# A graph layer's source gather: 48 of 420 columns made by TensorE instead of 39, named sooner, fetched a group ahead

## The reference, cut to what matters

```python
def _L1_gnn_ref(feat, W1, W2, b, src, dst):
    out_deg = jnp.maximum(segment_sum(ones, src), 1.0)
    t1 = feat @ W1
    msg = t1[src] + feat[src] * feat[dst] @ W2
    msg = msg / (sqrt(out_deg[src]) * sqrt(out_deg[dst]))[:, None]
    agg = jax.ops.segment_sum(msg, dst, num_segments=n)
```

## Time and profile before

| | us |
|---|---|
| median of three runs (lowest, highest) | 2574.71 (2570.63, 2580.15) |
| span of the profiled execution | 2204.9 |
| the stage of the change, from its first to its last sums | 1105.0 to 1596.8 |
| its first and last gather by GpSimd | 1105.7 and 1588.4 |
| its first and last matmul of L2323 | 1157.6 and 1592.5 |

### The profile page before, as it was taken

One profiled execution on the slowest core, in us unless ns is written; L12 is line 12 of the kernel. 1 busy time (PEld: TensorE's weight loads), 2 busy tenths in 40 slices (PEclk: granted clock), 3 DMA queues, 4 the chain that ended last, 5 costly groups with the idle time before them and its releaser, 6 DMA issues. The chain is left out here.

```text
span 2204.9 us, 38514 instructions
## 1 busy us (share of the span) xinstructions
PE 1760.4 (80%) x11779; PEld 1497.5 (68%) x11780; DVE 1277.6 (58%) x2754; ACT 873.7 (40%) x1797; POOL 1173.9 (53%) x1179
## 2 busy tenths in 40 slices
PE   5737988878775899699708878878778699999996
PEld 4525766666654777588607767666657599999995
DVE  7337977777768633346667788877638722222221
ACT  4425765555553244322142222222225634333332
POOL 2667777777770400056567777777640045444442
PEclk9958987777887899899959898999978699999998
DMA  3588655555565362567567866666650566767775
GB/s 93 137 181 199 169 162 151 154 156 150 157 150 131 79 181 80 140 198 226 181 192 248 263 225 224 222 219 219 214 157 24 181 208 192 203 187 192 199 188 146
DMA packets 203516, 384.67 MB, mean 174 GB/s; under 512 B 43525, under 2 KB 138170, under 8 KB 203199
## 3 DMA queue, kind: packets, MB, share of 16 engines
q1 hardware_dynamic: 136871, 223.77, 33.5%
q0 software_dynamic: 65696, 157.37, 26.8%
q10 hardware_dynamic: 840, 2.16, 0.3%
HBM read 277.93 MB, written 108.69 MB: 175 GB/s over the span
## 5 line engine op out<-in xcount | busy, mean ns | idle before, releaser
L808 POOL DMA_INDIRECT qr<-q_rows,src_t x415 | 407.4, 982 | 126.5 <-issue 124.1
L2303 POOL DMA_INDIRECT fr<-pair_rows,dst_i x381 | 363.0, 953 | 123.6 <-issue 113.1
L2323 PE MATMUL psP<-f_part,onehot 125*128 125x256 bf16 x2925 | 359.8, 286 | 85.2 <-DVE onehot L2349 85.1
L2323 PEld LDWEIGHTS psP<-f_part,onehot 125*128 125x128 bf16 x2925 | 297.2, 103 | 141.2 <-DVE onehot L2349 95.1
L906 PE MATMUL psK<-kp,oh_k 126*128 x1680 | 281.5, 332 | 94.1 <-DVE qr L1011 66.1
L906 PEld LDWEIGHTS psK<-kp,oh_k 126*128 126x128 bf16 x1680 | 191.4, 115 | 164.8 <-issue 99.8
L2361 DVE SCALAR_TENSOR_TENSOR psA<-psA,same,fr 128x256 f32<-128x256 f32 x420 | 206.5, 492 | 75.0 <-DMA fr<-pair_rows,dst_i 42.9
L2443 ACT ACTIVATE acc<-psA 128x1280 f32<-128x1280 f32 x84 | 103.9, 1237 | 331.0 <-DVEq L2364 310.8
L1919 ACT ACTIVATE m1hT<-m1psH,m1par 128x128 f32<-128x128 f32 x448 | 127.7, 368 | 252.7 <-PE m1psH L1939 252.7
L1939 PEld LDWEIGHTS m1psH<-m1xT,n_rows 128*128 128x128 f32 x1792 | 208.7, 192 | 5.0 <-DMA n_rows<-in_L_ffn_W_dram 1.2
L1939 PE MATMUL m1psH<-m1xT,n_rows 128*128 128x128 f32 x1792 | 209.3, 275 | 1.7 <-DMA n_rows<-in_L_ffn_W_dram 1.1
(11 more groups left out here) (502 smaller groups left out, 2685.1 us busy)
## 6 DMA issues: line engine op xcount, KB each, us to landing
n_rows<-in_L_ffn_W_dram SPq DMA_DIRECT2D x56, 1024.0 KB
run_rows<-acc SPq DMA_DIRECT2D x84, 640.0 KB
loc<-locals_ SPq DMA_DIRECT2D x85, 157.5 KB
ea<-in_edge_attr_dram SPq DMA_DIRECT2D x84, 140.0 KB
w_first<-in_L_ffn_Wd_dram SPq DMA_DIRECT2D x8, 1024.0 KB, 11.8
w_all<-in_L_ffn_W_dram SPq DMA_DIRECT2D x8, 1024.0 KB, 10.3
m1b<-in_L_ffn_b_dram SPq DMA_DIRECT2D x56, 128.0 KB, 2.9
qr<-q_rows,src_t POOLq DMA_INDIRECT x420
```

What stands on the lines that cost most here:

```text
L808: nc.gpsimd.indirect_dma_start(out=qr[:, n % GQ, u, :], out_offset=None, in_=q_rows, in_offset=bass.IndirectOffsetOnAxis(ap=src_t[:, n, u: ...
L2303: nc.gpsimd.indirect_dma_start(out=fr[:, n % GI, u, :], out_offset=None, in_=f_rows, in_offset=bass.IndirectOffsetOnAxis(ap=f_at[:, n * G ...
L2323: last = nc.tensor.matmul(psP[:, k % 2, 0:D], onehot[:, k % 2, t, :], f_part[:, c, t, :], start=(t == 0 and c == 0), stop=(t == T - 1 and ...
```

## The change

TensorE makes 48 columns. `PG` is now (7, 9, 10, 12, 14, 15, 17, 18, ..., 79, 80, 82): 28 of the distances between neighbours are two groups and 19 are one. Group 83 has no such column any more. Column k+1 is named after tile 6 of column k, not 12. ScalarE in turn n fetches the product for group n+1, if there is one, ahead of the copy of group n. The source numbers as floats lie in `dst_f`, a buffer that is free by then; one VectorE instruction makes them for all 84 groups, not for 39. The place of `one_hots` in VectorE's program, two groups ahead of use, is as before.

```diff
-        PG = tuple(range(7, NK, 2))
-        NP = len(PG)
+        NP = 48
+        PG = tuple(7 + (2 * i + 1) * (NK - 8) // (2 * NP) for i in range(NP))
-            cols7 = sb(st, "cols7", [E, NP])
+            cols7 = dst_f[:, 0:NK]
-                        if t == T // 2 and k + 1 < NP:
+                        if t == T // 4 and k + 1 < NP:
                             name_sources(k + 1)
-                nc.vector.tensor_copy(cols7[:], src_i[:, PG[0] * G + G - 1::2 * G]).then_inc(s_cols7, 1)
+                nc.vector.tensor_copy(cols7[:], src_i[:, G - 1::G]).then_inc(s_cols7, 1)
-                    nc.scalar.activation(col_wide[:, k % CR, :], cols7[:, k:k + 1].to_broadcast([E, P]), ACT.Copy).then_inc(s_colb, 1)
+                    nc.scalar.activation(col_wide[:, k % CR, :], cols7[:, PG[k]:PG[k] + 1].to_broadcast([E, P]), ACT.Copy).then_inc(s_colb, 1)
                 for n in range(NK):
-                    if n in PG:
-                        k = PG.index(n)
+                    if n + 1 in PG:
+                        k = PG.index(n + 1)
                         if k + 3 < NP:
                             widen(k + 3)
                         act.wait_ge(s_pe7, k + 1)
-                        act.wait_ge(s_free7, n - GI + 1)
-                        nc.scalar.activation(fr[:, n % GI, G - 1, :], psP[:, k % 2, 0:D], ACT.Copy).then_inc(s_pek7, 1)
+                        act.wait_ge(s_free7, n + 1 - GI + 1)
+                        nc.scalar.activation(fr[:, (n + 1) % GI, G - 1, :], psP[:, k % 2, 0:D], ACT.Copy).then_inc(s_pek7, 1)
```

## The result

| | before | changed | |
|---|---|---|---|
| median of 17 runs each, us | 2574.71 | 2556.0 | ratio 0.9926, 95% interval 0.9906 to 0.9947 |
| lowest, highest | 2565.35, 2590.62 | 2543.6, 2586.45 | |
| forecast | | 2565.4 (2557 to 2581) | |

The changed kernel's highest time is of a slow run, which the ratio leaves out. The mechanism that the prediction gave is not the one at work.

The account below looks back on a forecast made before the run. GpSimd's gathers were taken to bound the stage, ending it at 1583.9, the VectorE-TensorE chain at 1583.5; with 2 us added, 1585.9 against 1595.25 is 9.3 us less: 2574.7 becomes 2565.4 us, range 2557 to 2581.

Parts of the forecast that it names:

- With the 369.8 us around it as before: Last step, whole kernel: 369.8 us outside the span stay, so a span of 2195.6 us gives a median of 2565.4.
- It waits for nobody ... GpSimd is saturated.: Stage of the change: GpSimd's gathers cost 1.256 us each and set the pace; only 7.6 us are waits for VectorE.
- the 11.3 of the sum: GpSimd in the stage: nine gathers go at 1.256 us each, 11.3 us, with no cover.
- A column is 8.41 us.: TensorE in the stage: 8.41 us from naming to naming with nothing waited for, naming included.
- The early name: VectorE's one-hot: ready 6.2 us into a column, not 8.2, sparing VectorE 2 us in each of 19 places.
- The fetch ahead: ScalarE's fetch: removes VectorE's 9.0 us wait in 35 places, worth nothing before, needed now; possible delay taken as 0.
- nearly gone: Sign of being right, in the stage: VectorE's wait for the fetched column, 9.0 us in 35 places, nearly vanishes.
- those listed as wrong: Stage: GpSimd waiting for VectorE over 5 us beyond the start, mid-column naming waiting for fetch, copies awaiting TensorE, 10 us columns.
- those listed as right: Stage: 372 gathers with 0.30 us issue, last at 1577; VectorE's gather wait under 15 us; last sums at 1585 to 1587.
- A: Chain through VectorE and TensorE: 0.3 to 0.5 us per hand-over in 48 columns; 2582 us, at half 2573; chance 0.20.
- B's low clock: TensorE: 16 columns start at the low clock, 26.7 us on the chain; 15 us later than before, 2589.7; chance 0.10.
- C's wait for landed rows: Gathers in the stage: landing, not issue, sets the pace; gain 3 us, 2572; chance 0.10.

Follow-up runs that it names:

- before again: The kernel before, unchanged, profiled once more in the condition in which the change was timed; 2579.75 us beside 2582.2, ratio 0.9992.
- the second pair: The changed kernel against the same kernel without the fetch a group ahead (48 columns, named after tile 6); both 0.9926 of before, the latter 2568.78 us beside 2588.3.
- the waiting kernel: The changed kernel with GpSimd's gathers of group n waiting for TensorE's product of group n-2; 2217.17 us, 1.0011 of before, which took 2215.37 on that chip.

## Why the prediction was wrong

The step that failed is "With the 369.8 us around it as before", on which the reading of every row rests. In each of the runs here the device time is 1.7 to 2.1 us above the span of the same execution, so the 369.8 us between the median and the span of the first profile did not lie around it. It meant that the profiled execution ran at another pace than the timed ones, and that the rows described a condition in which the change was not going to be timed. Most of the rest follows.

- **"It waits for nobody ... GpSimd is saturated."** True of the profile read, and at that pace the price of a gather held within a fifth (44.0 against 39.9 to 43 us, 28.9 against 24 to 26). In the timed condition GpSimd waits 156.3 us for VectorE. Nine gathers less with the name as before (48 columns only) gave 7 us, 0.3 to 13.7; this does not exclude the 11.3 of the sum.
- **"A column is 8.41 us."** From first to last matmul it is 8.3 us in the median of the first profile, 13.0 in before again (27 of 39 over 11), 11.1 in the changed kernel (25 of 48), and 8.3 with one gather a group.
- **The early name, taken at 0 beside columns a group apart** (it only kept 2 us in 19 places from being lost). This is the mis-sized step behind the gain: alone it gave 19 us (12.7 to 25.3), as much as the change.
- **The fetch ahead, at 0.** Right in size: 0.9999 alone, and the ratio is 0.9926 with and without it. The prediction also called it needed in a tight chain; that the second pair doesn't show.
- **VectorE's wait for fetched columns "nearly gone".** It rose, 90.3 to 123.6 us. Its wait for gathers did fall below 15 us, but it was so in before again too.
- **The signs.** Of those listed as wrong, three stand in the profile after: GpSimd waits for VectorE (147.5 us, bound 5), columns of 10 us and more (11.1 in the median), and a naming that waits for the fetch in the middle of a column (25.5 us in nine places, and 60.7 us with the early name alone). Of those listed as right: 372 gathers with 0.28 us of "issue" each, but the last at 1921.9.
- **The rivals.** None was this. A (a price at each hand-over) is nearest in kind, but its sign was the other: in the timed condition before paid such a price already, and the change pays less of it (VectorE waits 206.3 us for names and products in before again, 150.0 in the changed kernel). B's low clock has a part, but is not the cause: in before again matmuls that follow each other at about twice the full-speed distance add 51 us to the columns (27 in the first profile), the stalls of over 0.5 us 176, and with one gather a group two of these stalls are left. The earlier trace rows already had a full-speed column behind a wait of 2.76 us, so a wait of over 2.1 us does not decide it alone. C's wait for landed rows is in neither profile of this pace.

So the right sign was luck: it came of a wrong model, and the gain of a part that the sum had at 0. What stays open: by what path the gathers hold TensorE back; whether TensorE's matmuls or only the signals are late in a stall (both kinds of rows are above); why one kernel takes 2215 us on one chip and 2580 on others; whether the changed kernel gains its 11 us at the faster pace; and whether holding GpSimd back helps at the slower one.

## What to carry to other kernels

Compare the profiled execution's span with the timed median before using a row: here a gap of 14% meant that another condition was timed, and its waits had to be profiled first. Where an engine stalls within its unit of work, move what others wait for to the front of the unit; here that was worth more than cutting the engine's work (19 us for the name, nothing for a third of the matmuls). A change of position tried as a series (tiles 18, 12, 6, 2) shows the cause as a dose, which a single edit does not.

## What the runs showed of the hardware

At the slower pace, TensorE's progress depends on GpSimd's indirect gathers. Some gathers after a pause its loads and matmuls come singly, in the stretch shown at multiples of 0.7 us; a column is 11.1 us (changed kernel) or 13.0 us (before again) long in the median, for 8.3. Late product signals arrive 2.8 us in the median (1.0 to 3.1, changed kernel) after the last gather began. With a quarter of the gathers all but two of 105 stalls are gone, and with rows an eighth as long they stay. At the faster pace gathers at the same rate do none of it: no late signal with 39, 16 or 4 columns, nor in the waiting kernel with 48.

Is TensorE short of instructions in these stalls? The Trainium skill (Runtime: NRT & Kernel Launch, "Instruction fetch mechanics") says that an engine fetches its instructions in blocks of 16 KiB by a DMA queue of its own, and that this is mostly hidden. The trace agrees with the blocks: one queue has 58 packets of kind "instruction" before, 37 with 4 columns and 64 with 48, of 16384 bytes each. As far as these packets show, the answer is no. In the gathers' stretch they took 1.07 us in the median in before again (23 packets) and 0.98 us in the first profile (24). None moves between 1543 and 1558, where the stall shown above lies. Of the 165 distances over 0.5 us between the loads of a column in before again, 8 have such a packet in flight; in the run named early only it is none of 124. When a fetch was asked for is not in the trace.

The Trainium skill also says (SBUF — State Buffer, "Who interferes with whom") that TensorE never waits on another engine at the memory's ports; no run here tests the ports. The 8.3 us against 11.1 shows that it is held back by GpSimd's gathers by some way, whether that one or not.
